# Attention loop: another split of PSUM banks between two rings, and the value product in one block

## The reference, cut to what matters

```
qkv = x @ Wqkv + bqkv
q, k, v = 32, 8, 8 heads of width 8        # k and v repeated 4 times
scores = q @ k.T / sqrt(8)
attn = softmax(scores)                     # over 512 keys
out = (attn @ v) @ Wo + bo
```

## Time and profile before

| | us |
|---|---|
| runs: median (lowest to highest of 3) | 675.0 (671.65 to 675.63) |
| the profiled execution | 669.68 |
| its span | 667.8 |
| TensorE busy | 617.4 (92%) |
| VectorE busy | 404.4 (61%) |
| ScalarE busy | 325.1 (49%) |
| attention loop, first scores to last turn of outputs | 362.19 to 565.55 |

### The profile page before, as it was taken

How to read it: one execution, slowest core, us unless ns; L and a number is a source line. 1 busy time by engine, 2 the same in 40 slices (tenths; PEclk the granted TensorE clock), 3 DMA queues, 4 the chain that set the end, 5 groups by cost and what they waited for, 6 DMA issues and landing times.

```text
span 667.8 us, 11795 instructions
## 1 busy us (share of the span) xinstructions
PE 617.4 (92%) x4298; PEld 408.0 (61%) x4298; DVE 404.4 (61%) x929; ACT 325.1 (49%) x645; POOL 213.2 (32%) x312
## 2 busy tenths in 40 slices
PE   3999999999999988799978999999999999989990
PEld 2887887887888785366665544444444445546660
DVE  4526705632760587533366999989998954743336
ACT  4523423433332224133215589898988875523322
POOL 5870561282073154513333031201010100331331
PEclk9999999999999999899989999999999999999996
DMA  6000200300199992222379994000000000031213
GB/s 220 33 1 33 96 1 20 107 1 1 38 283 299 78 314 77 78 58 81 105 237 346 303 180 3 1 1 2 2 1 2 1 2 1 9 104 55 81 56 126
DMA packets 69000, 57.40 MB, mean 86 GB/s; under 512 B 21520, under 2 KB 64400, under 8 KB 68944
## 3 DMA queue, kind: packets, MB, share of 16 engines
q1 hardware_dynamic: 66736, 50.60, 31.2%
q0 software_dynamic: 2208, 6.05, 2.5%
HBM read 30.78 MB, written 25.85 MB: 85 GB/s over the span
## 4 chain that ended last, share of the span: by engine, by line
PE 73%; DVE 16%; DMA 3%; ACT 3%; issue 2%; POOL 1%; SPq 1%; ACTq 0%; POOLq 0%; DVEq 0%
PE psum L303 9%; PE psum L305 8%; PE psum L304 8%; PE psum L1289 8%; PE psum L1634 8%; DVE mx L1744 7%; PE psum L1606 5%; PE psum L1318 5%; PE psum L1594 5%; PE psum L1619 3%; PE psum L1213 2%; DVE stat L666 2%; PE psum L1564 2%; PE psum L1282 2%; PE psum L1199 1%
## 5 line engine op out<-in xcount | busy, mean ns | idle before, releaser
L1744 DVE TENSOR_REDUCE mx<-psum 128x1 f32<-128x512 f32 x256 | 157.6, 681 | 17.6 <-PE psum L1606 17.5
L1505 ACT ACTIVATE pr<-psum 128x512 f32<-128x512 f32 x256 | 138.0, 598 | 27.9 <-PE psum L1619 26.1
L1634 PE MATMUL psum<-pr,vals 128*32 128x256 f32 x1024 | 77.6, 389 | 0.0
L1619 PE MATMUL psum<-qT,kT 32*128 32x512 f32 x256 | 76.6, 494 | 0.7 <-ACT pr L1505 0.7
L1606 PE MATMUL psum<-kT,qT 32*128 32x512 f32 x256 | 67.7, 488 | 1.7 <-ACT qT L1472 0.7
L1289 PE MATMUL psum<-w_gu,xgT 128*128 x120 | 56.4, 592 | 0.0
L624 POOL DMA_INDIRECT routed_y<-yr,xg x30 | 28.7, 958 | 86.1 <-DVE yr L876 85.5
L1606 PEld LDWEIGHTS psum<-kT,qT 32*128 32x128 f32 x256 | 26.3, 181 | 43.9 <-issue 21.4
L1546 POOL CAST mp<-mx 128x16 bf16<-128x16 f32 x16 | 3.1, 196 | 150.5 <-DVE mx L1744 150.5
L867 DVE SCALAR_TENSOR_TENSOR h<-psum,xg,sg 128x256 f32<-128x256 f32 x30 | 14.5, 484 | 49.8 <-ACT sg L1046 49.8
L1046 ACT ACTIVATE sg<-psum,xg 128x256 f32<-128x256 f32 x30 | 14.2, 474 | 60.4 <-PE psum L1289 60.4
(11 more groups left out here) (214 smaller groups left out, 1406.6 us busy)
## 6 DMA issues: line engine op xcount, KB each, us to landing
sorted_x<-zeros SPq DMA_DIRECT2D x2, 9088.0 KB, 39.2
w_gu<-in_L_ffn_gate_w SPq DMA_DIRECT2D x16, 256.0 KB, 6.2
w_gu<-in_L_ffn_up_w SPq DMA_DIRECT2D x16, 256.0 KB, 6.3
w_d<-in_L_ffn_down_w SPq DMA_DIRECT2D x16, 256.0 KB, 6.6
xg<-sorted_x SPq DMA_DIRECT2D x30, 129.0 KB, 2.2
wk_f<-in_L_attn_Wk SPq DMA_DIRECT2D x4, 512.0 KB, 5.2
wq_f<-in_L_attn_Wq SPq DMA_DIRECT2D x4, 512.0 KB, 6.0
wv_f<-in_L_attn_Wv SPq DMA_DIRECT2D x4, 512.0 KB, 3.7
```

The source lines that it names most:

```text
L1505: nc.scalar.activation(pr[d % 3][:, j], s2_bank(d, j), ACT.Exp, scale=SCALE).then_inc(exp_ready, 1)
L1619: mm(s2_bank(d, j), kT[n // GH][rows, kc * P:(kc + 1) * P], qT2[n % 2][rows, :], start=True, stop=True).then_inc(s2_made, 1)
L1634: last = mm(ps[AV_BANK][j * VW:(j + 1) * VW, cols], vals[:, n // NKV * TB + kc, n % NKV // GH * GH + j, :], pr[d % 3][:, j, cols], start=( ...
L1744: v.tensor_reduce(mx[n % 2][:, t, j:j + 1], s1_bank(c, j), AX.X, ALU.max, negate=True).then_inc(max_read, 1)
```

## The change

It has three parts. Bank 5 goes from the ring that VectorE reads to the one that ScalarE reads: DVE_BANKS become 0, 1, 2 and ACT_BANKS 3, 4, 5, 7. `weigh` does all 512 columns of a head in one matmul, where it did 256 columns for four heads and then the other 256, and it stands at the end of a step; before, its first half stood between the two pairs of scores in three steps of four. The turn of outputs stands behind the last pair of scores, before the value product; before, it stood ahead of them. In ScalarE's ring the late outputs follow the step's four scores, as TensorE now does them.

```diff
--- before.py
+++ after.py
@@ -1358,7 +1358,7 @@
         PROJ_BANK = [ps[2]] * TB + [ps[i] for i in (2, 3, 5, 6)]
         QKV_BANK = (4, 5, 6, 7, 3, 4, 6, 6)
         QKV_AT = 3
-        DVE_BANKS, ACT_BANKS = (0, 1, 2, 5), (3, 4, 7)
+        DVE_BANKS, ACT_BANKS = (0, 1, 2), (3, 4, 5, 7)
         HEADS2 = (2, 3, 0, 1)
         AV_BANK, TURN_BANK = 6, 7
 
@@ -1396,7 +1396,8 @@
                 FOR_DVE += [x_ for x_ in new if x_[0] == "o"]
             if c_ >= LAG:
                 S2 = [("s2", s2_no(c_ - LAG, j)) for j in HEADS2] if c_ < STEPS + LAG else []
-                FOR_ACT += S2[:2] + [x_ for x_ in new if x_[0] != "o" or x_[1] >= LATE_O] + S2[2:]
+                FOR_ACT += S2[:2] + [x_ for x_ in new if x_[0] != "o"] + S2[2:]
+                FOR_ACT += [x_ for x_ in new if x_[0] == "o" and x_[1] >= LATE_O]
 
         SPARE = [i for i in ACT_BANKS if all(ACT_BANKS[FOR_ACT.index(("o", n)) % len(ACT_BANKS)] != i
                                              for n in range(LATE_O, NG))][0]
@@ -1619,22 +1620,20 @@
                     mm(s2_bank(d, j), kT[n // GH][rows, kc * P:(kc + 1) * P], qT2[n % 2][rows, :], start=True,
                        stop=True).then_inc(s2_made, 1)
 
-            def weigh(d, half):
+            def weigh(d):
 
                 n, kc = d // TB, d % TB
                 pe.wait_ge(exp_ready, (d + 1) * GH)
-                if half == 0 and kc == 0:
+                if kc == 0:
                     pe.wait_ge(vals_ready, n // NKV + 1)
                     if n == 0:
                         pe.wait_ge(qkv_ready, NT)
                     if n:
                         pe.wait_ge(oT_ready, n)
-                cols = slice(half * S // 2, (half + 1) * S // 2)
                 for j in range(GH):
-                    last = mm(ps[AV_BANK][j * VW:(j + 1) * VW, cols], vals[:, n // NKV * TB + kc, n % NKV // GH * GH + j, :], pr[d % 3][:, j, cols],
-                              start=(kc == 0 and half == 0), stop=(kc == TB - 1), skip_group_check=True)
-                if half:
-                    last.then_inc(av_done, 1)
+                    last = mm(ps[AV_BANK][j * VW:(j + 1) * VW, :], vals[:, n // NKV * TB + kc, n % NKV // GH * GH + j, :], pr[d % 3][:, j, :],
+                              start=(kc == 0), stop=(kc == TB - 1), skip_group_check=True)
+                last.then_inc(av_done, 1)
 
             def turn_att(t):
 
@@ -1684,28 +1683,24 @@
                     keep_warm(2, 3)
                 if 0 <= d < STEPS:
                     scores2(d, 0)
-                if 0 <= d - 2 < STEPS and (d - 2) % TB:
-                    weigh(d - 2, 0)
                 for what in turns_at(c):
                     if what[0] != "o":
                         turn(what)
                 if c < STEPS:
                     scores1(c, 1)
-                for what in turns_at(c):
-                    if what[0] == "o":
-                        if what[1] == NG - 1:
-                            keep_warm(2, SPARE)
-                        turn(what)
                 if c < QKV_AT:
                     keep_warm(2, 3)
                 if 0 <= d < STEPS:
                     scores2(d, 1)
                 if QKV_AT <= c < QKV_AT + TB:
                     project_qkv(TB + c - QKV_AT)
+                for what in turns_at(c):
+                    if what[0] == "o":
+                        if what[1] == NG - 1:
+                            keep_warm(2, SPARE)
+                        turn(what)
                 if 0 <= d - 2 < STEPS:
-                    if (d - 2) % TB == 0:
-                        weigh(d - 2, 0)
-                    weigh(d - 2, 1)
+                    weigh(d - 2)
                 if 0 <= c - PROJ_AT < TB:
                     turn_att(c - PROJ_AT)
                 if 1 <= c - PROJ_AT <= TB:
```

## The result

| | us |
|---|---|
| before: median (lowest to highest of 20 runs) | 672.22 (669.69 to 677.29) |
| changed: median (lowest to highest of 20 runs) | 676.55 (672.23 to 680.84) |
| ratio, 95% interval | 1.0063 (1.0041 to 1.0086) |
| profiled execution, changed | 679.83, span 678.0 |

The change makes the kernel 0.6% slower, some 4.2 us: no change by the bound of 1%, but its interval leaves equality out. The forecast was 1.7 us slower.

A forecast was written before the change was run, and what follows sets the result against it. TensorE, busy 92%, and VectorE's maxima take turns; afterwards a loop through head 0's maximum sets the step. Terms +1.8, +0.7, +2.9 and -3.7 give +1.7 us: 676.7 on a median of 675.0, range 668 to 685.

The forecast's parts named there:

- The loop inside the step: Attention loop: head 3's score waits for head 0's maximum, starting 1.26 to 1.27 us after head 0's; steps 2.70, outputs' step 3.44.
- The merged value product at 1.00: Value product at the step's end: 1.00 us taken, between bounds 0.86 and 1.14.
- the rival at 1.14: Merged value product costs its two halves apart, 1.14 us: +8.4 over 60 steps, 685 us; chance 0.13.
- Groups: Steps 9 to 60, 13 groups of four steps: 11.54 us each, 150.0 against 148.22, +1.8.
- fits in 2.70: ScalarE's four exponentials and a copy in a step, 2.5 us, were said to fit in the step's 2.70.
- 0.26 until the turn binds: Turn of queries or keys, between the score pairs: costs nothing, binds next if maxima were quicker by more than 0.26 us.
- Steps 61 to 63: The loop's steps 61 to 63: 8.1 us against 7.41, +0.7.
- Start: First steps of the loop, four of them projecting the second batch's queries, keys and values: +2.9 us in all.
- the 0.81 from a score to its maximum behind a projection: In projection steps VectorE adds the bias first, so the next step's first maximum starts 0.81 us after its score.
- End: Tail without maxima, where the fourth bank and the merge pay: -3.7 us.
- about 1.0: Tail: the last value products save about 1.0 us, up to where the last exponentials hold them.
- The rule on repeated gaps: Repeated gaps can mean too few buffers: the fourth bank would pay back 7.6 us of one stretch; judged to speak equally against.

The follow-up runs named there:

- Experiment 5: Changed kernel with maxima taken over only the first 256 of a score's 512 columns; ratio to before 0.9865, 662.68 us.
- experiment 3: Changed kernel with the value product as two 256-column halves, one right behind the other at the step's end; ratio to before 1.0088, 679.32 us.
- experiment 4: Changed kernel with three filler matmuls on the identity between the score pairs of steps 0 to 3 (before two, none in step 3); ratio to before 1.0043, 675.82 us.
- experiment 1: Kernel before with the bank split alone, three for VectorE and four for ScalarE, order and halves as before; ratio 1.0398, 699.64 us.
- experiment 2: Changed kernel with the banks of before, four for VectorE and three for ScalarE; ratio to before 1.0263, 690.13 us.

## Why the prediction was right, and where its terms were off

The result, 676.55, lies on the forecast of 676.7; but the forecast was set on a median of 675.0 from three runs, and over 20 the kernel before is at 672.22. As a difference it was 1.7 forecast and 4.2 (2.8 to 5.8) measured. So the close meeting of the two values is luck: a base 2.8 too high and a difference 2.5 too low cancel. What was right is the mechanism, and that the change stays within 1%. By its own steps:

- **The loop inside the step**: right. Head 3's score starts 1.27 after head 0's, the value product 0.43 later, the steps are 2.70 to 2.73 and 3.45. Experiment 5 shortens the maximum by 0.27 and the steps it sets by 0.26 to 0.43.
- **The merged value product at 1.00**: right, and the rival at 1.14 is out (experiment 3 shows that the form of the block does not count either).
- **Groups**: +1.8 forecast, 11.62 x 13 = 151.1, so +2.8 at a full clock. The sum of the chain was 0.01 to 0.03 us a step short. For the two steps with a turn of queries the cause is known: I wrote that ScalarE's work "fits in 2.70", from its total, and did not follow its ring as I did VectorE's. Its loop closes at 1.30, just behind the other, and also takes the place of the "0.26 until the turn binds": nothing was to be had there (experiment 5).
- **Steps 61 to 63**: 8.14 (544.95 to 553.09) against 8.1.
- **Start**: +2.9 forecast, +2.3 measured at a full clock: the first eight steps take 23.20 against 20.82 (experiment 3), and the ninth 3.13 (experiment 4) against 3.22. That the filled start of experiment 4 took 26.83 and the forecast was 26.9 is luck, since 0.5 of it is the fill. The term that was off is the 0.81 from a score to its maximum behind a projection. I read it from a step before, where VectorE came late to the bias. With three banks VectorE is idle there and waits for the projection; the maximum starts 0.58 after the score (373.77 to 374.35), and 0.58 + 0.68 + 0.05 + 0.43 + 1.49 is the measured 3.23, not 3.46. What I left out is that the clock can fall here: 31.33 in the changed kernel's profile. I had read the granted clock of the loop, 1.00, as something that stays.
- **End**: -3.7 forecast. From step 61 the changed kernel takes 29.46 against 31.45, less the 0.7 that was counted apart: -2.7. The step that failed is the last item, "about 1.0" for the last value products. Before, the last scores of step 69 to the last turn took 4.84 us (560.71 to 565.55), now 4.58 (569.47 to 574.05): 0.26, since the last block waits for the last exponentials. The second step with a turn of outputs gained 0.3 in place of 0.5. The two steps of 3.47 became 2.67 and 2.71, as forecast.

So the mechanism was right. Three terms were off, by +1.0 in the groups, +1.0 at the end and -0.6 in the start, which makes 3.1 us at a full clock. The rest up to 4.2, 1.1 in the mean of the runs, can be the clock; that is not shown.

The rule on repeated gaps, of the Trainium skill (Perfetto Trace Analysis, Identifying Performance Opportunities), points at a real lack, but on both sides: experiments 1 and 2 show each ring, with its three banks, as the one that binds when the order is not fitted to it (12.0 and 12.5 us a group).

## What to carry to other kernels

When a ring of buffers loses one, write down for each item which item frees it, and look whether that one has moved into the same step of the loop: then a round trip through the other engine lies on the step, and all that is queued behind the waiting instruction pays for it. Do so for every ring, also for the one that gains; totals that fit don't show a loop. Before a duration is taken from a trace, look whether the engine was behind there: the 0.81 us held only while VectorE had a backlog, and was 0.58 without it. Buffers and order belong together: each half of this change is slower alone, and where the two are chosen for each part of the loop (start, middle, end), the same pieces are 0.9% faster than before.

## What the runs showed of the hardware

- A fall of the granted clock to the 1.2 GHz level can cost more than the waits of a change, and executions of the same code differ in it: the first eight steps of the loop took 27.67 us at 0.81 in the changed kernel's profile and 23.20 at 1.00 in that of experiment 3, which has the same instructions there. Busy time does not tell it: the loop of the changed kernel keeps 1.00 with TensorE 92% busy, and experiment 1 falls to 0.92 over 13 groups with TensorE 97% to 98% busy.
- Four column strips of fp32 matmuls take 1.00 us to the next scores as 16 records of 256 columns or as 8 of 512, and 1.14 as two blocks of 8 apart (0.57 each): so it is standing apart that costs, 0.14, and not the form of the block. That it is the going over between differently split uses of the array that costs this is my reading; no run here parts it from other causes.
